# Perceiver kernel on one core: the first cross-attention's loop holds 16 batches a pass instead of 8

## The reference

```python
q = split_heads(queries @ Wq + bq)          # queries = layernorm(x), 16 heads of width 8
k = split_heads(keys @ Wk + bk)             # keys = values = ctx, 257 rows a batch
v = split_heads(values @ Wv + bv)
scores = jnp.einsum('bhqd,bhkd->bhqk', q, k) / jnp.sqrt(jnp.float32(HD))
scores = jnp.where(mask, jnp.float32(-1000000000000000.0), scores)
attn = jax.nn.softmax(scores, axis=-1)
ctx = jnp.einsum('bhqk,bhkd->bhqd', attn, v)
return ctx.transpose(0, 2, 1, 3).reshape(b, sq, d) @ Wo + bo
```

## Time and profile before

| | |
|---|---|
| runs | 2444.99 us (2444.36 to 2445.66) |
| profiled execution, its own time | 2440.65 us |
| its span, first to last instruction | 2438.7 us |
| busy: PE, DVE, ACT, POOL | 2083.5, 1634.8, 1427.0, 457.9 us |
| mean granted TensorE clock | 0.929 |

### The profile page before, as it was taken

One profiled execution on the slowest core, in us unless ns is written; L12 is line 12 of the kernel. 1 busy time (PEld: TensorE's weight loads), 2 busy tenths in 40 slices (PEclk: granted clock), 3 DMA queues, 4 the chain that ended last, 5 costly groups with the idle time before them and its releaser, 6 DMA issues. The chain is left out here.

```text
span 2438.7 us, 77682 instructions
## 1 busy us (share of the span) xinstructions
PE 2083.5 (85%) x25732; PEld 1603.5 (66%) x25771; DVE 1634.8 (67%) x5601; ACT 1427.0 (59%) x3597; POOL 457.9 (19%) x1078
## 2 busy tenths in 40 slices
PE   5999999997988998999999999996556025699999
PEld 3878888875763677999999999995134013444454
DVE  4777777776755235877777787786989877631311
ACT  4888888886743115655555555555677577532322
POOL 2555555552300840000000000000000030000000
PEclk9999999998979999999999999997988555899999
DMA  3222222220012824565556556552000000100000
GB/s 90 81 76 79 75 77 73 77 70 4 0 29 60 164 58 114 120 129 122 106 121 131 109 109 131 120 109 70 0 1 0 0 2 3 49 5 5 9 4 13
DMA packets 266731, 158.07 MB, mean 65 GB/s; under 512 B 40560, under 2 KB 256512, under 8 KB 266240
## 3 DMA queue, kind: packets, MB, share of 16 engines
q1 hardware_dynamic: 266624, 156.65, 27.9%
HBM read 135.34 MB, written 21.23 MB: 64 GB/s over the span
## 5 line engine op out<-in xcount | busy, mean ns | idle before, releaser
L1195 ACT ACTIVATE c_PR<-c_PR,c_nmx 128x257 f32<-128x257 f32 x512 | 252.8, 496 | 69.8 <-DVE c_nmx L1242 69.8
L1238 DVE CUSTOM_DVE_ANT_0 c_PR<-c_b,c_MB 128x257 f32<-128x257 f32 x512 | 195.1, 424 | 125.4 <-PE c_b L1120 118.5
L684 ACT ACTIVATE a_PR<-a_SM,a_nmx 128x257 f32<-128x257 f32 x512 | 253.3, 499 | 4.1 <-POOL a_XL L459 3.6
L1131 PE MATMUL c_b<-c_PT,c_C 32*128 32x128 f32 x8192 | 238.8, 272 | 3.7 <-ACT c_QP L1188 2.1
L1131 PEld LDWEIGHTS c_b<-c_PT,c_C 32*128 32x128 f32 x8192 | 232.3, 187 | 7.9 <-issue 4.3
L1120 PE MATMUL c_b<-c_cT,c_QP 128*128 128x257 f32 x1024 | 230.5, 383 | 0.8 <-ACT c_QP L1188 0.8
L731 DVE CUSTOM_DVE_ANT_0 a_SM<-a_bs,a_MB 128x257 f32<-128x257 f32 x512 | 188.0, 423 | 60.4 <-PE a_bs L552 33.5
L1120 PEld LDWEIGHTS c_b<-c_cT,c_QP 128*128 128x128 f32 x1024 | 191.9, 190 | 31.2 <-issue 2.8
L1255 DVE STREAM_TRANSPOSE c_PT<-c_PR 128x256 f32<-128x256 f32 x512 | 181.4, 412 | 0.0
L1200 ACT ACTIVATE c_OT<-c_b 128x512 f32<-128x512 f32 x128 | 76.4, 597 | 169.0 <-PE c_b L1131 169.0
L1088 POOL TENSOR_TENSOR c_XL<-quarter,c_PR 128x16 f32<-128x16 f32 x128 | 27.6, 216 | 660.8 <-DVE c_PR L1250 660.8
(11 more groups left out here) (496 smaller groups left out, 4804.1 us busy)
## 6 DMA issues: line engine op xcount, KB each, us to landing
c_C<-in_ctx_dram SPq DMA_DIRECT2D x512, 128.0 KB, 3.1
a_C<-in_ctx_dram SPq DMA_DIRECT2D x128, 128.0 KB, 2.1
ctxT_dram<-a_cT SPq DMA_DIRECT2D x128, 128.0 KB, 1.8
f_RWB<-f_rw_dram SPq DMA_DIRECT2D x16, 1024.0 KB, 13.5
c_cT<-ctxT_dram SPq DMA_DIRECT2D x128, 128.0 KB, 3.2
a_MK<-in_mask_Bx1xSxS_bk_dram SPq DMA_DIRECT2D x128, 32.1 KB, 1.9
X<-in_x_dram SPq DMA_DIRECT2D x4, 512.0 KB, 6.4
g_h<-in_L_ffn_h_w_dram SPq DMA_DIRECT2D x2, 1024.0 KB, 6.9
```

What stands on the lines that cost most here:

```text
L684: nc.scalar.activation(PR[:, 1 - par, hg, :], SM[:, 1 - par, hg, :], ACT.Exp, bias=nmx[:, 1 - par, hg:hg + 1], accum_out=den[:, 1 - par, h ...
L1131: last = nc.tensor.matmul(banks[:, h, 0:P], C[rows, b, kb, :], PT[rows, b, kb, :, :], start=(kb == 0), stop=(kb == NKB - 1), tile_position ...
L1195: nc.scalar.activation(PR[:, b, hg, :], PR[:, b, hg, :], ACT.Exp, bias=nmx[:, b, hg:hg + 1], scale=SCALE, accum_out=den[:, b, hg:hg + 1]). ...
L1238: nc.vector.tensor_tensor_reduce(PR[:, b, hg, :], banks[:, hg, 0:SK], MB[:, :], 1.0, NEG1, ALU.add, ALU.max, mx[:, b, hg:hg + 1]).then_inc ...
```

## The change

A constant `U = 16` takes the place of the 8 in the three parts of every engine's stream: batches 0 to 15 are straight code, the loop has passes 1 to 6 with 16 batches each, and the last 16 batches (with the emptying steps) are straight code again. So 6 passes run where 14 ran, and the numbers that are derived from the pass counter (tile, semaphore values) are scaled. Nothing else differs: which instruction follows which on an engine when the program runs, buffers, waits and DMAs are the same.

```diff
@@ -301,6 +301,7 @@
     SCALE = HD0 ** -0.5
+    U = 16
@@ -378,13 +379,13 @@
-            for g in range(8):
+            for g in range(U):
                 one(g, g, g // 4, lambda lag, g=g: (g + lag) // 4)
-            with eng.Fori(1, B // 8 - 1) as j:
-                for r in range(8):
-                    one(8 * j + r, r, 2 * j + r // 4, lambda lag, j=j, r=r: 2 * j + (r + lag) // 4)
-            for g in range(B - 8, B + extra):
-                one(g, g % 8, g // 4, lambda lag, g=g: (g + lag) // 4)
+            with eng.Fori(1, B // U - 1) as j:
+                for r in range(U):
+                    one(U * j + r, r, U // 4 * j + r // 4, lambda lag, j=j, r=r: U // 4 * j + (r + lag) // 4)
+            for g in range(B - U, B + extra):
+                one(g, g % U, g // 4, lambda lag, g=g: (g + lag) // 4)
@@ -631,17 +632,17 @@
-            with pe.Fori(1, B // 8 - 1) as j:
-                for r in range(8):
-                    s = Step(8 * j + r, r, B)
-                    s.tile, s.fours = 2 * j + r // 4, lambda lag, j=j, r=r: 2 * j + (r + lag) // 4
-                    s.ctx = 32 * j + 16 * ((r + 2) // 4 + 1)
-                    s.values = 16 * j if r < 6 else 16 * j + 16
+            with pe.Fori(1, B // U - 1) as j:
+                for r in range(U):
+                    s = Step(U * j + r, r, B)
+                    s.tile, s.fours = U // 4 * j + r // 4, lambda lag, j=j, r=r: U // 4 * j + (r + lag) // 4
+                    s.ctx = 4 * U * j + 16 * ((r + 2) // 4 + 1)
+                    s.values = 2 * U * j + 16 * ((r - 6) // 8 + 1)
                     step(s)
...
```

More of the change, by code:

```diff
@@ L446, in step @@
                         wait(pool, m_in[(r + 1) // 4 % 2], s.masks)
-                    prepare(g + 1, (r + 1) % 8)
+                    prepare(g + 1, (r + 1) % U)
                 if s.on(1):
@@ L486, in one @@
                 step(s)
-            for g in range(8):
+            for g in range(U):
                 one(g, g, g // 4, lambda lag, g=g: (g + lag) // 4, 64 * (1 + (g + 1) // 8))
-            with pool.Fori(1, B // 8 - 1) as j:
-                for r in range(8):
[L491 to L494, removed]
+            with pool.Fori(1, B // U - 1) as j:
+                for r in range(U):
+                    one(U * j + r, r, U // 4 * j + r // 4, lambda lag, j=j, r=r: U // 4 * j + (r + lag) // 4,
+                        U * 8 * j + 64 * (1 + (r + 1) // 8))
+            for g in range(B - U, B + 3):
+                one(g, g % U, g // 4, lambda lag, g=g: (g + lag) // 4, 64 * (1 + (g + 1) // 8))
         @block.tensor
@@ L633, in _ @@
             turn(1, 1, 16)
-            for g in range(8):
+            for g in range(U):
                 one(g, g, g // 4, lambda lag, g=g: (g + lag) // 4)
-            with pe.Fori(1, B // 8 - 1) as j:
-                for r in range(8):
-                    s = Step(8 * j + r, r, B)
-                    s.tile, s.fours = 2 * j + r // 4, lambda lag, j=j, r=r: 2 * j + (r + lag) // 4
-                    s.ctx = 32 * j + 16 * ((r + 2) // 4 + 1)
-                    s.values = 16 * j if r < 6 else 16 * j + 16
+            with pe.Fori(1, B // U - 1) as j:
+                for r in range(U):
+                    s = Step(U * j + r, r, B)
+                    s.tile, s.fours = U // 4 * j + r // 4, lambda lag, j=j, r=r: U // 4 * j + (r + lag) // 4
+                    s.ctx = 4 * U * j + 16 * ((r + 2) // 4 + 1)
+                    s.values = 2 * U * j + 16 * ((r - 6) // 8 + 1)
                     step(s)
-            for g in range(B - 8, B + 3):
-                one(g, g % 8, g // 4, lambda lag, g=g: (g + lag) // 4)
+            for g in range(B - U, B + 3):
+                one(g, g % U, g // 4, lambda lag, g=g: (g + lag) // 4)
         @block.scalar
```

## The result

The changed kernel takes 2452.58 us (median of 9 runs, 2446.16 to 2460.66) against 2444.99 us (9 runs, 2442.03 to 2445.99) of the kernel before on the same chip. The ratio is 1.0034, with a 95% interval from 1.0019 to 1.0049: 8.3 us slower, between 4.6 and 12. The forecast of 2449.1 us has the right sign and lies 3.5 us short; the measured median stands at the very edge of the forecast's own range (2446.6 to 2452.6), 0.02 us inside it, which is luck. The case "slower by over 0.2%" came true; it had 0.35, "within 0.2%" had 0.52.

What follows compares the result with a forecast made beforehand. PE was busy 500.04 of 502.00 us but not taken as sole pacer, with ACT at 87%. -4.6 + 0.2 + 8.5 = +4.1 us on 2440.65 gave 2444.8, and 4.3 to the median 2449.1 us; own range 2446.6 to 2452.6.

Steps and rivals of the forecast that it cites:

- slower by over 0.2%: Outcome case for the whole kernel: a time over 2449.9 us; chance 0.35.
- within 0.2%: Outcome case for the whole kernel: neither under 2440.1 us nor over 2449.9; chance 0.52.
- Boundaries and straight code (-4.6 + 0.2 us): First cross-attention loop: eight pass boundaries fewer at 0.58 us, 4.6 us less; sixteen more straight batches, 0.2 us more.
- it arises on ACT: At a pass boundary: 0.39 of the 0.58 us shows on ACT, between the sums' copy and the first exponential.
- More pages to bring, cost nothing: Longer code of the loop: 9 more pages for PE and 11 for the others, brought once without a stall.
- DVE and ACT miss at each of 5 branches, side by side: Loop's branches back: bodies of 4 pages miss on both engines, stalls count once, 8.5 us in all; chance 0.52.
- The price of a miss (1.7 us): Stall at a branch back into missing code: 1.7 us, between 1.2 and 3.4.
- PE at nothing: PE's loop body touches 7 pages, 31 instructions short of an eighth, and still fits; cost nothing.
- the page beginnings: Instruction stream: PE's pages begin at 192 (within 3) plus multiples of 256, the others' at 64 plus multiples of 128.
- Rival B: Loop's branches back: misses cost two latencies, 3.4 us each, as if PE misses too; +12.6 us, 2457.6 us; chance 0.15.

Runs made afterwards that it cites:

- e4: The changed kernel with DVE back at 8 batches a pass and 12 empty instructions ahead of ACT's loop; 2437.34 us.
- e6: The changed kernel with no loop in the first cross-attention, all 128 batches as straight code on all five engines; 2434.37 us.
- e8: The changed kernel with only ACT at 16 batches a pass, 12 empty instructions ahead of its loop, the other engines back at 8; 2441.53 us.
- e1: The changed kernel with ACT back at 8 batches a pass, the other engines at 16; 2446.87 us.
- e5: The changed kernel with DVE back at 8 batches a pass and 80 empty instructions ahead of ACT's loop; 2457.62 us.
- e2: The changed kernel with DVE back at 8 batches a pass, the other engines at 16; 2453.27 us.
- e11: The changed kernel with ACT and DVE back at 8 batches a pass and 150 empty instructions ahead of PE's loop; 2510.69 us.
- e7: The changed kernel with ACT and DVE back at 8 batches a pass and 50 empty instructions ahead of PE's loop; 2448.57 us.
- e9: The changed kernel with PE at 32 batches a pass, ACT and DVE back at 8, POOL and SP at 16; 2443.31 us.
- e10: The changed kernel with only PE at 16 batches a pass, the other engines back at 8; 2441.66 us.
- e3: The changed kernel with ACT and DVE back at 8 batches a pass, PE, POOL and SP at 16; 2439.66 us.

## Why the prediction was right, and where it wasn't

1. **Boundaries and straight code (-4.6 + 0.2 us).** The size held: e4, where the longer passes fit, is 496.1 - 500.6 = -4.4 us in the phase, with DVE still at 8; e6 gains 6.5. The reason did not: "it arises on ACT" was read from a wait next to the boundary, and e8 refutes it. What the earlier trace rows show on ACT is its own branch, which PE's hides.

2. **More pages to bring, cost nothing.** Right: e6 brings 83 and 106 packets and is the fastest.

3. **DVE and ACT miss at each of 5 branches, side by side.** Right, with the rows named for it: q14 in every pass, q8 silent, ACT's idle time grown (3.09 us instead of 0.29). e1 to e5 show it in both directions.

4. **The price of a miss (1.7 us).** This term was too small. ACT's sequencer goes on 2.4 to 3.1 us after the branch and DVE's 2.8 to 3.1, where it took 0.24 to 0.27 and 0.32 to 0.34. Per branch the phase lost (511.4 - 496.1) / 5 = 3.05 us: against e4's 62.95 us, the five stretches with a branch lost 2.7, 2.7, 4.9, 2.8 and 2.3 us. The one of 4.9 follows the longest stall of ACT (3.1 us): there ACT waits once more, 0.81 us for PE (`a_bs`), 7.9 us behind the branch, and batch 48 lasts 5.95 us, where the first batch of the next pass lasts 4.05. Such a wait of 0.8 us stands once in e2 and once in e5 too, each time in the dearest stretch; what brings it isn't shown. The estimate took the landing of one 8 KB load (1.6 us) for nearly the whole. In e2, where the pages are ACT's alone, 0.9 to 1.2 us go by from the branch until the first page moves, near the 0.8 to 1.0 of the estimate, and another 1.5 to 2.0 us until ACT's next instruction, though the page itself moves for 0.3 to 0.8 us; that last part the estimate lacked. 5 x 3.05 = 15.2 in place of 8.5 makes -4.4 + 15.2 = +10.8 us in the phase, which is what it shows.

5. **PE at nothing.** Right, and so were the page beginnings: seven pages, 31 instructions short of an eighth (e11's second wait). The margin was wider than it looked, since e7 went some 20 instructions into the eighth page at no cost. Rival B doubted this margin, and its price for PE would have been too small: a miss there costs 6 to 9 us.

6. **The sum.** The span grew by 8.7 us and the phase by 10.8. The phases behind it gave the rest back little by little (the end of the first layer's feed-forward is 10.9 us later, that of the second self-attention 9.9). No experiment aimed at this. From the first maximum of batch 127 to the end of the span, where all thirteen kernels have the same work, the profiled executions take 1884.4 (the changed kernel) to 1890.1 us, 1886.8 before, so it is of the size by which executions differ; it stays open. So does the spread of the changed kernel's runs, 14.5 us against 4.0 before. Stalls of 2.4 to 3.1 us and a wait of 0.8 us that comes or doesn't would give such a spread, and e2, where ACT misses too, has 11.1 us, but only one execution of each was profiled. By the phase alone the prediction was 6.7 us short (+4.1 against +10.8): sign, place and count of the misses were right, and the total came out nearer to the forecast than the phase by scatter.

The Trainium skill's page "Runtime: NRT & Kernel Launch", section "Instruction fetch mechanics", gives a store of 512 instructions for most engines and 2048 for PE, and a window of two pages for a branch. The runs agree with the sizes: on ACT three pages of 128 stay in place and a fourth misses (e4, e5), which is the store less one page; on PE seven of 256 stay, and eight, the whole store, stay or miss by how far the last is used (e7, e11). They contradict the window: PE branched back over seven pages with no packet.

## What to carry to other kernels

Before unrolling a loop further, count the pages its body touches on each engine, and where it begins: here up to 3 pages of 128 instructions on ACT and DVE and 7 of 256 on PE came back free. A fourth page cost 2.3 to 3.2 us a branch on ACT and 1.7 on DVE, and eight and fourteen pages on PE cost 9.3 and 6.2 (except in e7, which barely entered its eighth). If a body touches one page too many by a few instructions, moving its start can be enough (12 empty instructions, 16 us). Where it misses, the next page should not begin right behind the branch's target: there a second wait came (e2, e11) that e5 and e9 don't have. If it doesn't fit at all, straight code was better than a long loop here, since code that runs forward came in without a stall.

## What the runs showed of the hardware

- A branch back costs something even when its target is held: 0.24 to 0.34 us on ACT and DVE until the next instruction. PE's compare-and-branch itself takes 0.21 us when it is taken (0.08 when not), and the next instruction follows 0.06 us behind. It is PE's that the pass shows (e8, e10). At a miss PE's branch lasts 3.9 to 4.8 us.
- When one page more than fits is touched, not one page is fetched but all of the body and one more: 5 packets a branch for 4 pages on ACT or DVE, 9 for 8 on PE (e11), 15 for 14 (e9). A loop that is just too long loses all its pages; a store in which the oldest page goes first would do that, but only the count is shown.
- A miss on PE is dearer than one on ACT or DVE (6.2 to 9.3 us a branch against 1.7 to 3.2). The first three pages came about 4 us apart behind each branch of e11.
- Empty semaphore increments aren't free: in the traces they follow each other at 0.15 us on PE (e7, e11) and 0.07 on ACT (e4, e5). 50 ahead of PE's loop moved the phase's start by 9.6 us (e7 against e3), 80 ahead of ACT's by 7.1 us (e5 against e2).
